# x transposes move two halves ahead into slots 7 and 8, q projections into slots 0, 3 and 5

## The reference

```
q = heads(x @ W_q);  k_t, v_t = heads(text @ W_k), heads(text @ W_v)
probs_t = softmax(q k_t^T * 16**-0.5);  text_out = probs_t v_t
qsem = l2norm(probs_t @ text);  sem = qsem . l2norm(ip)
probs_ip = softmax(q k_ip^T * 16**-0.5 + 0.5 * sem) * spatial_mask
out = (text_out + probs_ip v_ip) @ W_out + b_out + x
```

## Time and profile before

| | |
|---|---|
| median of 3 runs | 343.29 us (342.98 to 343.63) |
| profiled execution | 343.5 us |
| its span | 341.8 us, granted clock 1.000 |
| TensorE busy | 317.8 us (93%) |
| VectorE busy | 292.4 us (86%) |
| ScalarE busy | 290.9 us (85%) |
| GpSimd busy | 139.5 us (41%) |

### The profile page before, as it was taken

One profiled execution on the slowest core, in us unless ns is written; L12 is line 12 of the kernel. 1 busy time (PEld: TensorE's weight loads), 2 busy tenths in 40 slices (PEclk: granted clock), 3 DMA queues, 4 the chain that ended last, 5 costly groups with the idle time before them and its releaser, 6 DMA issues.

```text
span 341.8 us, 9000 instructions
## 1 busy us (share of the span) xinstructions
PE 317.8 (93%) x2344; PEld 296.8 (87%) x2344; DVE 292.4 (86%) x2010; ACT 290.9 (85%) x1241; POOL 139.5 (41%) x301
## 2 busy tenths in 40 slices
PE   3999988899999999999999999999999999999974
PEld 3797857789998989899999999899999998989863
DVE  5656647899999999999999999999999999999973
ACT  2836678899999999998999999999999999999951
POOL 3033410454554454445444445354554554322241
PEclk9999999999999999999999999999999999999999
DMA  7950003001102020202011120202021102100001
GB/s 213 344 142 0 2 20 69 3 2 30 59 21 61 28 61 19 61 23 59 28 25 36 30 61 19 60 29 60 19 61 32 59 19 61 30 20 21 21 21 58
DMA packets 14618, 16.99 MB, mean 50 GB/s; under 512 B 2080, under 2 KB 14024, under 8 KB 14568
## 3 DMA queue, kind: packets, MB, share of 16 engines
q1 hardware_dynamic: 14568, 16.42, 16.0%
HBM read 10.55 MB, written 5.24 MB: 46 GB/s over the span
## 4 chain that ended last, share of the span: by engine, by line
PE 79%; ACT 12%; DVE 6%; issue 1%; DMA 1%; SPq 0%
PE gv_ps L837 21%; PE mi_ps L801 13%; PE mi_ps L872 12%; PE et_ps L824 11%; PE sc_ps L816 10%; ACT e_sb L481 6%; ACT qs L473 3%; PE mi_ps L783 2%; PE gv_ps L950 2%; PE mi_ps L850 1%; DMA place_ctx<-in_ctx 1%; DVE place_ctxT L624 1%; PE mi_ps L785 1%; DVE ktok L672 1%; PE sc_ps L930 1%
## 5 line engine op out<-in xcount | busy, mean ns | idle before, releaser
L481 ACT ACTIVATE e_sb<-sc_ps,negmax 128x60 f32<-128x60 f32 x640 | 147.7, 322 | 14.6 <-DVE negmax L616 12.6
L837 PE MATMUL gv_ps<-tab,place_w 128*128 128x162 f32 x640 | 114.6, 301 | 0.4 <-ACT place_ctxT L490 0.4
L624 DVE CUSTOM_DVE_ANT_0 place_ctxT<-gv_ps,e_sb 128x60 f32<-128x60 f32 x640 | 99.9, 212 | 9.8 <-PE gv_ps L837 9.1
L837 PEld LDWEIGHTS gv_ps<-tab,place_w 128*128 128x128 f32 x640 | 94.2, 190 | 0.9 <-issue 0.8
L816 PE MATMUL sc_ps<-km,qs 128*128 128x256 f32 x320 | 77.3, 323 | 0.2 <-DVE qs L606 0.2
L429 POOL TENSOR_TENSOR mixed<-place_ctxT,rsum 128x320 f32<-128x320 f32 x32 | 23.8, 744 | 123.0 <-DVE rsum L731 123.0
L824 PE MATMUL et_ps<-ident,e_sb 128*128 128x128 f32 x320 | 63.9, 281 | 9.8 <-ACT e_sb L481 9.0
L494 ACT COPY place_w<-et_ps 128x256 f32<-128x256 f32 x160 | 63.7, 398 | 0.3 <-PE et_ps L824 0.3
L616 DVE TENSOR_REDUCE negmax<-sc_ps 128x4 f32<-128x240 f32 x160 | 63.6, 398 | 0.0
L824 PEld LDWEIGHTS et_ps<-ident,e_sb 128*128 128x128 f32 x320 | 38.0, 140 | 20.2 <-ACT e_sb L481 15.8
L624 DVE DVE_READ_ACCUMULATOR2_ANT quad<- 128x1 f32 x640 | 53.0, 83 | 0.0
(11 more groups left out here) (152 smaller groups left out, 537.5 us busy)
## 6 DMA issues: line engine op xcount, KB each, us to landing
x_nat<-in_x SPq DMA_DIRECT2D x16, 320.0 KB, 3.3
out<-place_w SPq DMA_DIRECT2D x32, 160.0 KB, 1.8
place_ctx<-in_ctx SPq DMA_DIRECT2D x4, 256.0 KB, 4.3
place_w<-in_L_xattn_W_v SPq DMA_DIRECT2D x1, 640.0 KB, 7.3
place_w<-in_L_xattn_W_k SPq DMA_DIRECT2D x1, 640.0 KB, 8.6
place_w<-in_L_xattn_W_k_ip SPq DMA_DIRECT2D x1, 640.0 KB, 10.0
place_w<-in_L_xattn_W_v_ip SPq DMA_DIRECT2D x1, 640.0 KB, 9.6
place_ctxT<-in_L_xattn_W_out SPq DMA_DIRECT2D x1, 640.0 KB
```

The source lines that it names most:

```text
L481: last = nc.scalar.activation(e_sb[:, slot, TOK * j:TOK * j + T], sc_ps[:, bank, TOK * j:TOK * j + T], ACT.Exp, bias=negmax[:, slot, j:j + 1])
L624: last = v.tensor_tensor_reduce(out=junk[:, u % 2, j, 0:T], in0=gv_ps[:, u % 2, TABW * j:TABW * j + T], in1=e_sb[:, u % ERING, TOK * j:TOK ...
L837: last = mm(gv_ps[:, u % 2, 2 * TABW * r:2 * TABW * r + 2 * TABW], eT[:, u % TRING, P * r:P * r + P], tab[:, b % 2, h:h + 2, :].rearrange( ...
```

## The change

The table of slots is written anew. x transposes are now made for the half two ahead of the running one, in slots 7 and 8; q projections still serve the next half, in slots 0, 3 and 5. "at" and "o" stay where they are. Transposes of half 1, which no slot makes any more, are put into the setup on TensorE, ScalarE and VectorE. The task that goes behind the table products of its slot (`early`) is now x 1 in slot 8. `MISC_ORDER`, and with it the bank and the waits of each task, follow the table.

```diff
@@ -233,21 +233,22 @@
 
 
 
-        MISC_SLOTS = {0: ("x", 0), 1: ("o", 1), 2: ("x", 1), 3: ("q", 0), 4: ("at", 0),
-                      5: ("q", 1), 6: ("o", 0), 8: ("q", 2), 9: ("at", 1)}
+        MISC_SLOTS = {0: ("q", 0), 1: ("o", 1), 3: ("q", 1), 4: ("at", 0), 5: ("q", 2),
+                      6: ("o", 0), 7: ("x", 0), 8: ("x", 1), 9: ("at", 1)}
         TASK_TILE = {("o", 1): -3, ("at", 0): -2, ("o", 0): -2, ("at", 1): -1}
+        TASK_HALF = {"q": 1, "x": 2}
 
         def misc_task(u):
 
             h, hu = divmod(u, UNITS // HALVES)
             kind, n = MISC_SLOTS.get(hu, ("", 0))
-            if kind in ("x", "q") and 0 <= h + 1 < ALL_HALVES and u >= 0:
-                return kind, n, h + 1
+            if kind in ("x", "q") and TASK_HALF[kind] <= h + TASK_HALF[kind] < ALL_HALVES:
+                return kind, n, h + TASK_HALF[kind]
             if kind in ("at", "o") and 0 <= 2 * h + TASK_TILE[kind, n] < ALL_TILES - 1:
                 return kind, 0, 2 * h + TASK_TILE[kind, n]
             return "", 0, 0
 
-        MISC_ORDER = [("x", 0, 0), ("x", 1, 0), ("q", 0, 0), ("q", 1, 0), ("q", 2, 0), ("v", 0, 0)]
+        MISC_ORDER = [("x", 0, 0), ("x", 1, 0), ("q", 0, 0), ("q", 1, 0), ("q", 2, 0), ("v", 0, 0), ("x", 0, 1), ("x", 1, 1)]
         MISC_ORDER += [misc_task(u) for u in range(ALL_UNITS + UNITS) if misc_task(u)[0]]
 
         def misc_bank(task):
@@ -533,6 +534,8 @@
             exps(1)
             act.wait_ge(pre_v, PAIRS)
             nc.scalar.copy(v_sb[:, PAIRS - 1, :], mi_ps[:, 1, 0:C]).then_inc(v_copied, 1)
+            x_hi(1, 0)
+            x_hi(1, 1)
             copy_eT(0)
             for n in range(6):
                 rows = 96 if n < 5 else B
@@ -691,6 +694,8 @@
                     vip[:, :, 0:NDIF].unsqueeze(2).to_broadcast([rows, B, hp, NDIF]),
                     head_of_row[0:rows, 0:hp].unsqueeze(1).unsqueeze(3).to_broadcast([rows, B, hp, NDIF]),
                     ALU.mult).then_inc(vip_made, 1)
+            x_low(1, 0)
+            x_low(1, 1)
             maxima(2)
 
             def attnT_lows(t):
@@ -968,6 +973,8 @@
             last.then_inc(pre_vip, 1)
             pe.wait_ge(q_lo, 2)
             v_product(PAIRS - 1, mi_ps[:, 1, :])
+            x_transposes(1, 0)
+            x_transposes(1, 1)
             pe.wait_ge(zeros_made, 6)
             e_transposes(0)
 
@@ -1004,7 +1011,7 @@
                         pe.wait_ge(u_lo_made, index // TILES + 1)
                     out_project(index, 1)
                 kind, n, index = misc_task(u)
-                early = (kind, n) == ("q", 0)
+                early = (kind, n) == ("x", 1)
                 if early and u < ALL_UNITS:
                     table_products(u)
                 if kind == "x":
```

## The result

The changed kernel takes 341.60 us in the median of 8 runs (339.86 to 343.08), the kernel before 343.15 (342.83 to 343.81): a ratio of 0.9942, 95% interval 0.9914 to 0.9970. It is faster, by 0.6%, where 345.4 us, slower than before, had been forecast: the measured time moved the other way. Once more on another chip it was 340.39 against 343.17, ratio 0.9918 (0.9888 to 0.9948). The two kernels' lines differ by 1 to 5: L824 (transposes of e) is L829 after, L481 L482, L466 L467, L598 L601, L742 L747, L872 L877.

The account below looks back on a forecast made before the run. TensorE was taken to lead, VectorE and ScalarE only 4% behind. Setup and early halves +0.67, twelve full halves +2.3, half 14 -0.8 and half 15 -0.1 made +2.1 us: 345.4 against the median, range 340.8 to 347.5.

Parts of the forecast that it names:

- What bounds the kernel, and where the waits sit: TensorE leads, other engines 4% behind; late exponentials stall it ahead of slot 5 (0.44 us), a late maximum ahead of slot 1.
- New waits: Late ScalarE exponentials stall TensorE: 0.34 us ahead of slot 2, 0.19 ahead of slot 9, 0.31 ahead of next slot 0.
- The prices of small instructions: Engine times taken from the old trace: x0's high part 0.54 us, logarithm 0.25, x1's high part 0.27, ipmax 0.26.
- The walk: Pieces laid on three engines through one half in the new order: 17.98 us, 18.31 with u_all, mean 18.15 against 17.95.
- u_all: ScalarE's 0.36 us copy in slot 2 of every second half now delays slot 5: half 18.31 instead of 17.98.
- before, the copy was hidden: In the old kernel ScalarE waited for q0 anyway, so the 0.36 us copy of u_all was hidden.
- Twelve full halves: Halves 2 to 13 take 217.74 us against 215.41 before: +2.3 us.
- Savings of 0.6 a half: Per half, stalls of 0.44 and 0.15 us and smaller waits go, but 0.34 + 0.19 + 0.31 replace them.
- the widest range: Total time from 340.8 us, half of the faster rival's cases, up to 347.5; likeliest 345.4.
- the first rival: Faster: gaps close, none open, VectorE doesn't idle ahead of x1's low part; 17.5 a half, 337.7 us; chance 0.20.
- Ends: Setup 1.0 us longer, 0.35 given back, so +0.67 at half 2; half 14 -0.8, half 15 -0.1.
- The x load: Load issued in slot 3 lands in time, 4 us spare; rival where it lands 2 us late: 367 us, chance 0.03.

Follow-up runs that it names:

- the variant: Kernel after with x1's low part on VectorE behind the products and ipmax of its slot instead of ahead of them: 339.49 us, 0.9881; on another chip 339.02, 0.9882.
- the waits filled: Idle identity transposes where TensorE waits in the last 12 us: kernel after 341.31 us (0.9930); with x1's low part behind ipmax and u_all's copy moved, 340.77 and 339.06.

## Why the prediction was wrong

- *What bounds the kernel, and where the waits sit*: right. The stall ahead of slot 5 is gone (slot 4 is 1.38 instead of 1.94 in even halves), that ahead of slot 1 too.
- *New waits*: right in kind, wrong in size. The forecast put 0.34 + 0.19 + 0.31 into slots 1, 8 and 9; they measure 0.05, 0 and 0.41 (slot 9 1.81 against TensorE's own 1.40). VectorE does wait for x1's high part, 0.23 instead of 0.53, and lags at slot 0 by 0.21 instead of 0.45. The order with x1's high part behind the exponentials made that lag larger and lost 9 us, the one with its low part behind ipmax took it away and gained 1.
- *The prices of small instructions*: here the forecast failed. These are the terms from which the new stalls were worked out. It took the time from one start to the next beside one neighbour and used it beside another. Logarithm behind x0: with x0 0.61, not 0.79. ipmax ahead of a maximum: 0.15, not 0.26; ahead of a low part it is 0.27 in the variant too. x1's high part ahead of exponentials or a copy, both from PSUM: 0.40, not the 0.27 ahead of the logarithm. Each sits on the chain that goes from ScalarE's slot 8 over VectorE's slot 9 to slots 0 and 1, so an error is paid more than once: -0.19 in slot 8, +0.10 in slot 9, -0.29 in slot 1. The walk had been held against the rows of before only at the starts of slots 1, 2 and 5, and not at slots 8 and 9, where this chain begins. The Trainium skill, "Perfetto Trace Analysis", Optimizing Scalar/DVE Operations, says of the fixed data access of each instruction that its profiled latency is about twice the time for which it keeps the engine busy, since the half in which the write is acknowledged overlaps with the next instruction. These rows agree in part: ipmax, 0.23 long, holds VectorE for 0.15, but x1's high part, 0.37 long, holds ScalarE for 0.40.
- *u_all*: the step "before, the copy was hidden" was wrong: moving it in the kernel before took 0.15 off slot 3 of odd halves. After, it costs 0.22 in slot 4, not 0.35, and slot 5 gives 0.09 back. Odd halves are longer than even ones by 0.15 before and 0.14 after, so the change costs nothing here, where the forecast had 0.33 in each of six halves, 2.0 of its +2.3 us.
- *Twelve full halves*: +2.3 us forecast, -1.9 measured. All of the wrong sign is here. Savings of 0.6 a half stood against costs of 0.8, and the difference was taken as surer than 0.1 a half; the prices alone were off by 0.1 to 0.2 each. The 0.1 us a half either way that the forecast allowed was too narrow by more than a factor of three: it was 0.36. That the measured 341.6 lies within the widest range, 340.8 to 347.5, is due to the part of the first rival that was taken in; that rival's path is not what happened, since the lag and the wait ahead of x1's low part stayed.
- *Ends*: right, and a bit on the careful side. Setup: from the start of v's last group (L930, L935) to the first transposes of e 1.54 us instead of 0.59, 0.95 more against a forecast 1.0; with halves 0 and 1 it is +0.73 at the start of half 2 against +0.67; half 14 16.79 against 17.1.
- *The clock at the end*: not in the forecast at all. It falls in the kernel before as well: 22 of the 82 executions of it beside the experiments have a mean clock under 0.996, with spans of 342.4 to 344.8 where the others have 340.2 to 342.8, and 6 of 16 of the kernel after. So it widens both and is no cause of the gain. With the waits filled it was 0 of 21. Over all executions without filled waits it was 41 of 178; at that share 0 of 21 would come by chance in 0.4% of cases, an estimate from these counts. That the idle waits bring it about is what these runs point to. It isn't all: it was also 0 of 10 in each of two kernels with idle waits, and the profiled run before kept 1.00 through them; what decides it stays open.
- *The x load*: no wait for it appears in the table of waits, as forecast.

## What to carry to other kernels

When a hand order moves work between slots of engines whose busy times are within 5% of each other, write the walk down as a range: the sum of what closes and the sum of what opens are each larger than their difference, and a price that is taken beside one neighbour can be off by half beside another. Follow the lag of the second engine out of the half, since it is paid again at the beginning of the next one, and look at what stands behind each moved piece on its engine, as attention's low part stood behind u's. A stall on the busiest engine is not by itself worth closing: the order that took half of the largest one away lost 9 us.

## What was not expected of the hardware

u's low part on VectorE reads SBUF alone and is 0.49 us long in the kernel after. In the kernel after with the copy in slot 6 it stands beside GpSimd's product for mixed and is 0.75:

```profile
133.06 0.75 DVE L755 TENSOR_TENSOR u_all<-place_ctxT,u_all 126x320 fp32r<-126x320 f32 x1
```

```profile
132.72 0.74 POOL L430 TENSOR_TENSOR mixed<-place_ctxT,rsum 128x320 f32<-128x320 f32 x1 [3.68 <-DVE rsum L736]
133.44 0.56 POOL L435 TENSOR_SCALAR ipw<-iprec,mask_sb 128x20 f32<-128x20 f32 x1
```

All eight of them are 0.75 there, and in the kernel before with the same move, so a moved instruction also changes its own price by who runs beside it. GpSimd's ipw, 0.33 long in the median, is 0.56 here. The Trainium skill, "Perfetto Trace Analysis", Optimizing Scalar/DVE Operations, says that the two engines share a read port of SBUF; these rows fit that.

In the profiled run after, the granted clock was 1.00 (2.4 GHz) up to 330 us and fell to 1.2 GHz only in the thin end, where 7 us at the low level cost 2.35 us.
